# One-hots of the second graph layer's scores: ScalarE makes the destinations' half in two passes, VectorE the sources' half

## The reference

```
feat = h1 @ fc2_w.T                      # [3125, 256]
el, er = sum(feat * attn_l), sum(feat * attn_r)
e = leaky_relu(el[src] + er[dst], 0.2)   # one score per edge
a = softmax of e over the edges of one destination
h2 = segment_sum(feat[src] * a, dst) + bias
```

## Time and profile before

| | us |
|---|---|
| median of 3 runs | 2304.44 (2303.19 to 2308.76) |
| profiled execution, its own time | 2296.7 |
| its span in the trace | 2294.9 |
| TensorE busy | 1525.2 (66%) |
| VectorE busy | 1511.8 (66%) |
| GpSimd busy | 1275.2 (56%) |
| ScalarE busy | 417.4 (18%) |

### The profile page before, as it was taken

How to read it: one execution, slowest core, us unless ns; L and a number is a source line. 1 busy time by engine, 2 the same in 40 slices (tenths; PEclk the granted TensorE clock), 3 DMA queues, 4 the chain that set the end, 5 groups by cost and what they waited for, 6 DMA issues and landing times. The chain is left out here.

```text
span 2294.9 us, 29922 instructions
## 1 busy us (share of the span) xinstructions
PE 1525.2 (66%) x7823; PEld 1142.6 (50%) x7824; DVE 1511.8 (66%) x2311; ACT 417.4 (18%) x809; POOL 1275.2 (56%) x1321
## 2 busy tenths in 40 slices
PE   6347566675656445965666578877777666399965
PEld 5335444454536434754445434655555444377743
DVE  3357777777765876743333474777767767699968
ACT  1100000000013000000000053444443443100124
POOL 0477777777503887777777204677777774000023
PEclk9657778777878556987887799888778888599999
DMA  3644444444305664444444236899999997578512
GB/s 95 155 131 125 126 120 124 123 126 126 83 25 167 173 173 132 132 119 119 119 119 119 64 110 203 292 341 340 341 341 336 345 342 263 219 273 274 199 40 74
DMA packets 238176, 409.01 MB, mean 178 GB/s; under 512 B 33650, under 2 KB 174891, under 8 KB 231467
## 3 DMA queue, kind: packets, MB, share of 16 engines
q0 software_dynamic: 73216, 219.89, 31.2%
q1 hardware_dynamic: 164907, 188.55, 26.2%
HBM read 333.82 MB, written 74.48 MB: 178 GB/s over the span
## 5 line engine op out<-in xcount | busy, mean ns | idle before, releaser
L843 POOL DMA_INDIRECT row_space<-tab_feat,src_i x760 | 756.4, 995 | 302.6 <-issue 231.2
L1101 PE MATMUL ps<-arena 128*128 128x257 f32 (+1 forms) x1664 | 434.8, 423 | 151.1 <-DVE arena L1947 151.1
L843 POOL DMA_INDIRECT row_space<-tab_kv,src_i x416 | 393.5, 946 | 253.9 <-issue 123.7
L1101 PEld LDWEIGHTS ps<-arena 128*128 128x128 f32 x1664 | 344.8, 212 | 239.3 <-issue 177.8
L1941 DVE TENSOR_TENSOR arena<-row_space,ps 128x2048 f32<-128x2048 f32 x95 | 216.6, 2281 | 191.0 <-DMA row_space<-tab_feat,src_i 191.0
L1197 PE MATMUL ps<-arena 128*128 128x265 f32 x832 | 258.5, 477 | 115.4 <-DVE ps L2175 56.6
L1197 PEld LDWEIGHTS ps<-arena 128*128 128x128 f32 x832 | 194.8, 240 | 167.2 <-issue 123.1
L1041 PE MATMUL ps<-acc,arena 128*128 x832 | 272.3, 483 | 0.0
L1428 ACT COPY acc<-ps 128x265 f32<-128x265 f32 (+2 forms) x75 | 28.3, 377 | 1151.8 <-PE ps L1101 582.1
L1819 DVE TENSOR_TENSOR arena<-row_space,ps 128x1024 f32<-128x1024 f32 x104 | 126.8, 1219 | 137.3 <-PE ps L1041 92.8
L1041 PEld LDWEIGHTS ps<-acc,arena 128*128 128x128 f32 x832 | 189.1, 239 | 35.9
(11 more groups left out here) (335 smaller groups left out, 2185.1 us busy)
## 6 DMA issues: line engine op xcount, KB each, us to landing
item_v<-row_space SPq DMA_DIRECT2D x52, 1024.0 KB, 8.4
row_space<-item_v SPq DMA_DIRECT2D x52, 1024.0 KB, 4.9
arena<-rows_block_dst SPq DMA_DIRECT2D x104, 128.0 KB
row_space<-tab_feat,src_i POOLq DMA_INDIRECT x760, 2.8
scores<-rows_block_dst SPq DMA_DIRECT2D x52, 128.0 KB
arena<-rows_src_low SPq DMA_DIRECT2D x52, 128.0 KB
row_space<-tab_kv,src_i POOLq DMA_INDIRECT x416
arena<-rows_type SPq DMA_DIRECT2D x52, 128.0 KB
```

The costliest lines, as they stand in the source:

```text
L843: nc.gpsimd.indirect_dma_start(rows_of_slot(s)[:, g, :], None, table, bass.IndirectOffsetOnAxis(ap=src_i[:, item:item + 1], axis=0),).then ...
L1101: last = nc.tensor.matmul(ps[:, SUM_BANKS:2 * SUM_BANKS][:, bass.ds(bs[g], 1), 0:width].rearrange("p a d -> p (a d)"), onehot[:, s % 2, g, ...
```

## The change

In score2 VectorE's instruction is cut to the sources' half. ScalarE makes the destinations' half by Square and Relu, waiting for the copies, and for the products that read the slot before. A new pair of semaphores `dst_made` tells when it is done. SP's spread and TensorE's products wait for both; SP also raises a semaphore `spread_asked`, for which nobody waits. The copies, their sizes and the two slots stay as they are.

```diff
 def spread(u, s):
     sp.wait_ge(onehot_made[s % 2], nth(u, s) + (layer * HALF + 1))
+    if layer == 1:
+        sp.sem_inc(spread_asked, 1)
+        sp.wait_ge(dst_made[s % 2], nth(u, s) + 1)
+        sp.sem_inc(spread_asked, 1)
     for k in range(2):
...
-            for credit in slot_used + onehot_made + score_read + sort_row_used:
+            for credit in slot_used + onehot_made + score_read + sort_row_used + dst_made:
...
                         pe.wait_ge(onehot_made[s % 2], nth(u, s) + (layer * HALF + 2))
+                        pe.wait_ge(dst_made[s % 2], nth(u, s) + 2)
...
-            idle("score2")
+            begin(act, "score2", ["dve", "pe"])
+
+            def destination_onehots(u, s):
+
+                z = s % 2
+                act.wait_ge(bcast_in[z], nth(u, s) * 32 + (32 + broadcasts(1)))
+                act.wait_ge(score_mm[z], nth(u, s) + HALF)
+                did(nc.scalar.activation(onehot_t[:, z, 1], bcast[:, z, 1], ACT.Square, bias=minus_part_no[:]))
+                nc.scalar.activation(onehot_t[:, z, 1], onehot_t[:, z, 1], ACT.Relu, scale=-1.0,
+                                     bias=ones[:, 0:1]).then_inc(dst_made[z], 1)
+
+            with nc.scalar.Fori(0, TURNS) as u:
+                step.enter(u, SLOTS)
+                for s in range(SLOTS):
+                    destination_onehots(u, s)
+                step.leave(TURNS)
+            act.wait_ge(dst_made[1], HALF + 1)
+            end()
...
-                vec.tensor_scalar(onehot_t[:, z], bcast[:, z], part_no[:], None,
+                vec.tensor_scalar(onehot_t[:, z, 0], bcast[:, z, 0], part_no[:], None,
                                   ALU.is_equal).then_inc(onehot_made[z], 1)
```

More of the change, by code:

```diff
@@ L363, in graph_layers @@
         onehot_made = [sem(f"onehot_made{s}") for s in range(2)]
+        dst_made = [sem(f"destination_onehot_made{s}") for s in range(2)]
+        spread_asked = sem("item_rows_asked_for")
         score_mm = [sem(f"score_products_made{s}") for s in range(2)]
```

## The result

The changed kernel is slower: 2328.72 us (median of 6 runs, 2318.02 to 2329.31) against 2303.82 us (median of 6, 2294.55 to 2308.76). The ratio is 1.0103, with a 95% interval of 1.0080 to 1.0127, which is 24 us more, between 18 and 29. The forecast was +19.5 us, with 2311 to 2336 as the range.

A forecast was written before the change was run, and what follows sets the result against it. GpSimd's gathers bound the second sums; a slot's circle (2.34 + 0.15 + 0.04 + 0.43 + 3.43 = 6.39 us) ends score2 24.6 us later, which after 5.1 us of slack gives +19.5 us: 2324 us, range 2311 to 2336.

The forecast's parts named there:

- The bound: Second layer's sums: bound by GpSimd's gathers, 1.25 us each; the 137th needs the slot that group 6 frees.
- The slack of 5.1 us: Group 6's slot, freed at 927.1, wanted at 932.2: score2 may lengthen 5.1 us free, every us beyond delays the rest.
- The circle: One slot's turn in score2, passes, hand-over, issues and landing: 6.39 us forecast, setting the pace instead of an engine's load.
- the two passes: ScalarE's half in score2: 1.15 + 0.04 + 1.15 = 2.34 us against VectorE's 1.30, so the circle grows 1.04 us.
- The landing: Copies' time from second issue to landing in score2: 3.43 us forecast, as the two slots drift towards even distances.
- GpSimd's relief: Gathers in score2, less slowed by VectorE's shorter compare: a 21 us gain that turns into idle time, worth nothing.
- the signs: Expected in the trace: score2 gathers of 1.1 to 1.2 us on average, GpSimd idle some 40 us before one gather.
- A (VectorE's order): Rival, faster: VectorE's order sets score2's pace, the stage is 29 us shorter, time 2283.5; chance 0.06.
- B (short landings): Rival, no change: landings of 2.92 us give +6.9, of 2.64 zero; time 2304 to 2311; chance 0.11.
- C (slots in step): Rival, much slower: four copies always travel together, landing 4.30 us, circle 7.26, +41 us, time 2346; chance 0.08.

The follow-up runs named there:

- third_pass: The changed kernel with ScalarE's Square done twice, the same output written again; ratio 1.0216 to the kernel before.
- free_at_square: The changed kernel, but SP's copies wait for ScalarE's first pass, the only one that reads the bytes, instead of the second; ratio 0.9983 to the kernel before.
- before_split_compare: The kernel before with VectorE's compare of 128x2048 written as two of 128x1024, nothing on ScalarE; ratio 1.0008 to the kernel before.
- no_gathers_beside: The changed kernel, but GpSimd begins the second layer's gathers only when VectorE has ended score2; 2430.26 us in one execution.

## Why the prediction was right

**The bound.** GpSimd's stream sets the second layer's sums and the slot of group 6 is where score2 takes hold of it: right, seen in the 56.9 us wait, and moved in both directions by the experiments. VectorE's last multiplication that waits for a gather came at 1314.57 instead of 1284.04: 26.2 us of that arose after the first gather, where 19.5 were forecast, and 4.4 us are the later entry.

**The slack of 5.1 us.** Right. Score2 grew by 31.8 us and the 137th gather by 26.4, a difference of 5.4.

**The circle.** Its mechanism was right, its size 0.3 us too small. From the end of ScalarE's second pass for group 1 (737.51) to that for group 51 (904.36) 25 turns of slot 1 took 6.67 us each, against 6.39 forecast. The terms, measured as means over all groups after each slot's first:

| term | forecast | measured |
|---|---|---|
| ScalarE's start after the landing as VectorE sees it | 0 | 0.04 |
| the two passes | 2.34 | 2.33 |
| end of the passes to SP's first issue | 0.15 + 0.04 | 0.24 |
| to the second issue | 0.43 | 0.43 |
| landing | 3.43 | 3.63 |

The landing is the term that was most off. I let it fall with the distance between the two slots' copies. The distances did grow, to 3.0 us and more in 38 of 51 cases, but the landing was 3.59 us on average there, where it had been 3.44 before. Behind shorter distances it was 3.75, so the distance still counted; the level had risen. The prediction had no term for the gathers, which come faster once they are relieved. That gathers lengthen the landing is shown: it was 3.20 us without any, and fell to 3.02 in third_pass when they ended. That their rate explains the change is not shown, and one run speaks against it: with one gather per 1.67 us (before) the landing was 3.57 us over all distances, with one per 1.30 (changed) 3.63, but in free_at_square, with one per 1.33, the 13 landings behind distances of 3.0 us and more took 3.46 us, hardly more than before. Why the changed kernel's took 3.59 stays open.

The 0.28 us over 25 turns are 7 us of the trace, and account for the step from 24.6 to 31.8 us of score2. The time still came out within the range, since that had room for landings of up to 3.9 us.

**GpSimd's relief.** I gave it 21 us and no value. It was 30 us (37.7 us of excess down to 7.5) and had no value. So the signs that hang on it were off too: gathers of 1.00 us on average instead of 1.1 to 1.2, and a wait of 56.9 us instead of 40. I had priced the half compare at the whole 16.2 us of excess in sum1 of the kernel before. In that trace only 9.4 us of it, 0.19 us a compare, lie on gathers that end at the two distances from a compare's end that the last section gives; 4.6 us lie on gathers that end so behind other instructions of VectorE (L2152 and L2093).

**The rivals.** A (VectorE's order) fell: VectorE waited for a landing in all 52 groups. B (short landings): the shortest was 3.16 us. C (slots in step): the slots drifted apart from 2.2 us and the mean landing was 3.63.

## What to carry to other kernels

Where a buffer of two slots is refilled by DMA, add up its circle (reader, hand-over, issue, landing) before moving the reader to another engine. Work that runs in parallel on a free engine still lies in that circle, if it holds the buffer. Free the buffer at the last instruction that reads it, or give it more slots. And when a stage has two limits close to each other, here 5 us, price an edit at both: a relief at the one that isn't last is worth nothing until the other is moved too.

## What the runs showed of the hardware

- A GpSimd gather lost time to VectorE's compare by how the two met and not by the compares' total time. With two slots for the bytes, one compare of 1.3 us a group cost its gathers 0.72 us, two of 0.75 us cost 0.18 to 0.20, one of 0.75 us 0.14 to 0.18; with four slots the three figures are 0.81, 0.28 and 0.21.
- Where they met badly, the gather waited for the compare's end. In the changed kernel 38 gathers met one compare only, and began more than 0.1 us after it had begun: each ended 0.81 to 0.82 us after the compare's end. So did all 26 such gathers of the kernel before, whose compare is 1.3 us long. The Trainium skill (SBUF — State Buffer, "Who interferes with whom") says that the loser is blocked fully while the other holds the shared port pair; the trace agrees. A compare that began between 0.1 us before the gather's start and 0.45 us after it held the gather only until 0.12 us after the compare's own end, and that costs a gather of 0.95 us nothing when the compare ends 0.83 us into it or earlier. So a long compare costs far more than two halves of it. In the kernel before, a gather that began with a compare took 1.39 us:

```profile
820.53 1.29 DVE L1728 TENSOR_SCALAR arena<-arena,part_no 128x2048 bf16<-128x2048 uint8 x1 [0.77 <-DMA arena<-rows_block_dst]
...
820.54 1.39 POOL L843 DMA_INDIRECT row_space<-tab_feat,src_i  x1 [0.30 <-issue]
```

With the compare in two (before_split_compare) the gather lost nothing, although the two halves cover its whole length; that it gets its turn between them is an inference:

```profile
821.45 0.75 DVE L1728 TENSOR_SCALAR arena<-arena,part_no 128x1024 bf16<-128x1024 uint8 x1 [0.81 <-DMA arena<-rows_block_dst]
822.11 0.80 DVE L1729 TENSOR_SCALAR arena<-arena,part_no 128x1024 bf16<-128x1024 uint8 x1
...
821.45 0.94 POOL L843 DMA_INDIRECT row_space<-tab_feat,src_i  x1 [0.31 <-issue]
```

- VectorE pays too: its 0.75 us compare took 0.796 us on average beside gathers (changed kernel) and 0.753 without (no_gathers_beside).
- A copy of 128 KB from SP, the second of a pair, had landed for VectorE 3.20 us after its issue without gathers beside (no_gathers_beside), and after 3.63 us with them (changed kernel).
